# A transformer block on one core: second routing in groups of two tiles, and low weight pieces moved between engines

## The reference

```python
x = x + 0.5 * ffn(layernorm(x), gate, w0, w1, wo)     # first experts
x = x + attention(layernorm(x), ...)                  # 16 heads, latent queries, keys and values, rope
x = x + 0.5 * ffn(layernorm(x), gate, w0, w1, wo)     # second experts, the same weights

logits = x @ gate_kernel                              # 8 experts
w, idx = top_k(logits, 2); w = softmax(w)
inter = silu(x @ w0[e]) * (x @ w1[e])                 # 256 -> 512
out = sum over the two chosen e of w_e * (inter @ wo[e])
```

## Time and profile before

| | us |
|---|---|
| runs | 1121.5, 1124.51, 1124.83 |
| median | 1124.51 |
| profiled execution | 1126.85 |
| its span | 1125.0 |

### The profile page before, as it was taken

One profiled execution on the slowest core, in us unless ns is written; L12 is line 12 of the kernel. 1 busy time (PEld: TensorE's weight loads), 2 busy tenths in 40 slices (PEclk: granted clock), 3 DMA queues, 4 the chain that ended last, 5 costly groups with the idle time before them and its releaser, 6 DMA issues.

```text
span 1125.0 us, 22344 instructions
## 1 busy us (share of the span) xinstructions
PE 1046.2 (93%) x6294; PEld 819.3 (73%) x6295; DVE 714.6 (64%) x1570; ACT 522.0 (46%) x1127; POOL 442.8 (39%) x401
## 2 busy tenths in 40 slices
PE   4669999999889999999999999999989999999994
PEld 4558878887457777777777777777778558788883
DVE  6364665654457788877887887777244645655642
ACT  1243433432156677767677777667201034433321
POOL 2552223333334654645464634443014523223322
PEclk9999999999989999999999999999999899999998
DMA  9843544432100111111101111111644645544230
GB/s 243 269 163 78 134 102 107 103 55 34 57 0 24 44 39 39 38 39 38 34 25 39 38 39 39 38 38 58 216 145 164 205 139 118 146 102 107 45 56 7
DMA packets 71592, 95.82 MB, mean 85 GB/s; under 512 B 9600, under 2 KB 48640, under 8 KB 71296
## 3 DMA queue, kind: packets, MB, share of 16 engines
q1 hardware_dynamic: 57216, 78.04, 22.6%
q0 software_dynamic: 14304, 16.87, 8.7%
HBM read 64.37 MB, written 34.43 MB: 88 GB/s over the span
## 4 chain that ended last, share of the span: by engine, by line
PE 50%; DMA 27%; issue 10%; POOL 3%; DVE 2%; ACT 1%; POOLq 1%; SPq 0%; DVEq 0%; ACTq 0%
DMA out<-shared,small 13%; DMA x_after_moe<-shared,small 13%; PE bank L1632 10%; PE bank L1659 10%; PE bank L1620 5%; PE bank L1621 5%; PE bank L1622 5%; PE bank L1412 2%; PE bank L1607 2%; POOL rows_by_expert L533 2%; PE bank L1608 2%; PE bank L1739 1%; PE bank L1444 1%; PE bank L1446 1%; PE bank L1448 1%
## 5 line engine op out<-in xcount | busy, mean ns | idle before, releaser
L845 ACT ACTIVATE shared<-bank,small 128x512 f32<-128x512 f32 x256 | 176.5, 690 | 92.1 <-DVE small L1266 91.0
L1266 DVE TENSOR_REDUCE small<-bank 128x1 f32<-128x512 f32 x256 | 174.7, 685 | 45.3 <-PE bank L1622 45.0
L777 ACT CAST split_rows_and_inner<-bank 128x512 fp32r<-128x512 f32 x78 | 46.0, 589 | 246.7 <-PE bank L1429 246.7
L1632 PE MATMUL bank<-constants,shared 128*128 128x128 f32 x1024 | 156.1, 275 | 2.2 <-ACT shared L845 0.7
L1632 PEld LDWEIGHTS bank<-constants,shared 128*128 128x128 f32 x1024 | 122.3, 140 | 45.1 <-issue 13.8
L1446 PE MATMUL bank<-expert_weights_low,split_rows_and_inner 128*128 x312 | 143.3, 459 | 0.0
L1448 PE MATMUL bank<-expert_weights_high,split_rows_and_inner 128*128 x312 | 142.3, 456 | 0.0
L1444 PE MATMUL bank<-expert_weights_high,split_rows_and_inner 128*128 x312 | 124.7, 400 | 2.7 <-DVE split_rows_and_inner L1075 2.5
L1080 DVE TENSOR_TENSOR split_rows_and_inner<-bank,split_rows_and_inner 128x512 fp32r<-128x512 f32 x78 | 53.9, 691 | 113.6 <-ACT split_rows_and_inner L777 113.6
L1620 PE MATMUL bank<-expert_weights_high,shared_split 128*128 128x512 f32 x256 | 123.3, 482 | 1.4 <-POOL shared_split L589 1.4
L546 POOL DMA_INDIRECT x_after_moe<-shared,small x39 | 61.6, 1579 | 149.7 <-DMA x_after_moe<-shared,small 114.2
(11 more groups left out here) (189 smaller groups left out, 2165.2 us busy)
## 6 DMA issues: line engine op xcount, KB each, us to landing
expert_weights<-L_ffn_w_kernel SPq DMA_DIRECT2D x32, 512.0 KB, 5.0
shared<-rows_by_expert SPq DMA_DIRECT2D x78, 129.0 KB, 2.1
expert_weights<-L_ffn_wo_kernel SPq DMA_DIRECT2D x16, 512.0 KB, 6.4
shared<-inverse_sums SPq DMA_DIRECT2D x64, 128.0 KB, 2.9
attended_transposed<-shared SPq DMA_DIRECT2D x32, 256.0 KB, 3.1
expert_weights<-x_after_moe SPq DMA_DIRECT2D x8, 512.0 KB, 4.9
expert_weights<-attended_transposed SPq DMA_DIRECT2D x2, 2048.0 KB, 10.1
shared<-attended_transposed SPq DMA_DIRECT2D x2, 2048.0 KB, 11.6
```

The source lines that it names most:

```text
L845: nc.scalar.activation(prob[k % 4], bank[k % 4][:, :], ACT.Exp, bias=negmax[:, k % 8:k % 8 + 1], accum_out=psum[par][:, hh * GT + qt:hh * ...
L1266: V.tensor_reduce(negmax[:, k % 8:k % 8 + 1], bank[k % 4][:, :], AX.X, ALU.max, negate=True).then_inc(max_ready, 1)
L1632: last = tr(bank[4 + k % 2][:, c * P:(c + 1) * P], prob[k % 4][:, c * P:(c + 1) * P], ident)
```

## The change

The second routing goes by groups of two tiles (`GN = (4, 2)`): the transposes of group h and the ranks of the group before stand behind the projection of an even tile, the logits of the group before behind that of an odd one. `x2group` moves from `wraw` into the upper part of `wlo`, so that experts 0 and 1 are loaded as soon as the third group of four tiles is projected. ACT splits expert 0's high pieces around the last group's copies and expert 1's behind its exponential; DVE makes expert 0's low pieces within the last group's steps and expert 1's behind the tables, once the last rows are stored. In both expert stages the low piece of wo of experts 2 to 7 is made by POOL, behind the add before the change of expert. The norm of batch 1 moves behind the first two `ropes`. The counts of `keep_busy` change from 4, 5, 2, 16 to 3, 3, 2, 14. In the diff, slices to the group's size (`[:, 0:n]`) are left out.

```diff
@@ -33,6 +33,7 @@
+GN = (GT, 2)
...
@@ -145,7 +146,9 @@
+        wlo_at = -(-nc.sbuf_base // 32) * 32
+        wlo_plain = nc.alloc_sbuf_tensor_at("expert_weights_low_plain", [P, 2 * WEXP], F32, offset=wlo_at)
...
@@ -285,7 +288,7 @@
-        x2group = [late[:, PAIRS * S + k * GT * D:PAIRS * S + (k + 1) * GT * D].rearrange("p (a n) -> p a n", a=GT)
+        x2group = [wlo_plain[:, 2 * B * S + k * GT * D:2 * B * S + (k + 1) * GT * D].rearrange("p (a n) -> p a n", a=GT)
...
@@ -415,7 +419,7 @@
-                    sp.wait_ge(scattered[f][u], 16 * GT * TOPK * ((NG + 2 - u) // 3))
+                    sp.wait_ge(scattered[f][u], 16 * GN[f] * TOPK * ((NT // GN[f] + 2 - u) // 3))
...
@@ -426,7 +430,8 @@
-                sp.wait_ge(wlo_ready[f], 3)
+                sp.wait_ge(wlo_ready[f], 2)
+                sp.wait_ge(outer_low_ready[f], 1)
...
@@ -438,7 +443,8 @@
-                        sp.wait_ge(wlo_ready[f], e * 3)
+                        sp.wait_ge(wlo_ready[f], e * 2)
+                        sp.wait_ge(outer_low_ready[f], e)
...
@@ -477,7 +483,7 @@
-                    sp.wait_ge(xn_ready[2], g - 1)
+                    sp.wait_ge(xn_ready[2], (g - 1) * GT // GN[1])
...
@@ -505,11 +511,12 @@
                 if g + 2 < NG:
                     load_attended(g + 2)
                     load_x(g + 2)
+                elif g + 2 == NG:
+                    sp.wait_ge(wo_psum, (g + 1) * GT)
+                    load_expert(1, 0)
+                    load_expert(1, 1)
             for u in range(2):
                 sp.wait_ge(out_stored[u], 16 * NG // 2)
-            sp.wait_ge(xn_ready[2], NG)
-            load_expert(1, 0)
-            load_expert(1, 1)
             moe(1)
...
@@ -523,22 +530,33 @@
                 nc.gpsimd.tensor_tensor(rstd[:, bass.ds(at, count)], veps[:, bass.ds(at, count)],
                                         minus_half[:, 0:count], ALU.pow).then_inc(rstd_ready[n], 1)
-            def scatter(f, g):
+            def scatter(f, g, ks=range(TOPK)):
                 u = g % 3
                 pool.wait_ge(slots_ready[f], g + 1)
                 pool.wait_ge(xn_copied[f], g + 1)
-                for k in range(TOPK):
-                    for j in range(GT):
+                for k in ks:
+                    for j in range(GN[f]):
                         nc.gpsimd.indirect_dma_start(
                             out=xs, out_offset=bass.IndirectOffsetOnAxis(ap=slot[u][:, k, j:j + 1], axis=0),
                             in_=rows[u][:, j, k, :], in_offset=None).then_inc(scattered[f][u], 16)
             def add_results(f, dst):
+                def outer_low(e):
+
+                    par = e % 2
+                    pool.wait_ge(whi_ready[f], e * 3 + 3)
+                    nc.gpsimd.tensor_tensor(wlo[:, bass.ds(par * WEXP + 2 * WPIECE, WPIECE)],
+                                            wraw[:, bass.ds(par, 1), 2 * WPIECE:3 * WPIECE].rearrange("p a n -> p (a n)"),
+                                            whi[:, bass.ds(par * WEXP + 2 * WPIECE, WPIECE)].bitcast(F32),
+                                            ALU.subtract).then_inc(outer_low_ready[f], 1)
                 def turn(i):
                     for v in range(3):
+                        last = isinstance(i, int) and i * 3 + v == TILES - 1
+                        if not last:
+                            e = pool.value_load(split_tab[0:1, bass.ds(i * 3 + v + 1, 1)], min_val=0, max_val=E - 1)
                         pool.wait_ge(y_sb[f], i * 3 + v + 1)
                         prev = (v - 1) % 3
                         pool.wait_ge(added[f][prev], (i + (v > 0)) * 16)
...
@@ -548,10 +566,15 @@
                                 ap=tag[v][:, 1:2].bitcast(U32), axis=0),
                             in_=ysb[v], in_offset=None, bounds_check=T - 1, oob_is_err=False,
                             compute_op=ALU.add).then_inc(added[f][v], 16)
-
+                        if not last:
+                            with pool.If(e > 0):
+                                outer_low(e)
+
+                pool.wait_ge(tables_ready[f], 2)
                 turn(0)
-                with pool.Fori(1, TILES // 3) as i:
+                with pool.Fori(1, TILES // 3 - 1) as i:
                     turn(i)
+                turn(TILES // 3 - 1)
             pool.wait_ge(const_in, 48)
             for g in range(NG):
...
@@ -683,13 +706,15 @@
             multiply(NPAIR - 2, 0)
             multiply(NPAIR - 1, 1)
-            pool.wait_ge(veps_ready[2], 1)
-            root(2, 0, GT)
-            for g in range(NG):
-                if g + 1 < NG:
-                    pool.wait_ge(veps_ready[2], g + 2)
-                    root(2, 0, GT)
-                scatter(1, g)
+            for g in range(2):
+                pool.wait_ge(veps_ready[2], g + 1)
+                root(2, 0, GN[1])
+            for g in range(NT // GN[1]):
+                scatter(1, g, (0,))
+                if g + 2 < NT // GN[1]:
+                    pool.wait_ge(veps_ready[2], g + 3)
+                    root(2, 0, GN[1])
+                scatter(1, g, (1,))
             for u in range(2):
                 pool.wait_ge(out_stored[u], 16 * NG // 2)
             add_results(1, out.rearrange("b s d -> (b s) d"))
...
@@ -795,10 +823,6 @@
                             act.wait_ge(y_psum[f], t)
                             split_high(f, e, 2)
-                for e in range(0 if f == 0 else 2):
-                    act.wait_ge(w_in[f], 48 * 2)
-                    for piece in range(3):
-                        split_high(f, e, piece)
                 act.wait_ge(tables_ready[f], 2)
                 expert_steps(act, step)
                 it_high(TILES - 1)
...
@@ -914,10 +938,19 @@
                 pair(p, p % 2)
             take_inverse(NPAIR - 1)
-            for g in range(NG):
+            for g in range(NT // GN[1]):
+                last = g == NT // GN[1] - 1
+                if last:
+                    act.wait_ge(w_in[1], 48 * 2)
+                    split_high(1, 0, 0)
+                    split_high(1, 0, 1)
+                xt_out(2, g, xTr[1], logits_psum[1])
                 copy_rows(1, g)
-                xt_out(2, g, xTr[1], logits_psum[1])
+                if last:
+                    split_high(1, 0, 2)
                 choice_exp(1, g)
+            for piece in range(3):
+                split_high(1, 1, piece)
             moe(1)
...
@@ -944,71 +977,73 @@
-                for j in range(GT):
+                for j in range(GN[n // 2]):
-                dve.wait_ge(scattered[f][g % 3], g // 3 * (16 * GT * TOPK))
+                dve.wait_ge(scattered[f][g % 3], g // 3 * (16 * GN[f] * TOPK))
+                w = GN[n // 2] * P
-                V.tensor_copy(dst[:, 1, :], bank[1][:, :]).then_inc(xn_sb1[n], 1)
+                V.tensor_copy(dst[:, 1, 0:w], bank[1][:, 0:w]).then_inc(xn_sb1[n], 1)
+                u, n = g % 3, GN[f]
-                for j in range(GT):
+                for j in range(n):
-                for j in range(GT):
+                for j in range(n):
+                u, n = g % 3, GN[f]
...
@@ -1067,7 +1102,7 @@
-                                ALU.subtract).then_inc(wlo_ready[f], 1)
+                                ALU.subtract).then_inc((wlo_ready if piece < 2 else outer_low_ready)[f], 1)
...
@@ -1095,6 +1130,13 @@
                     dve.wait_ge(y_psum[f], t + 1)
                     dve.wait_ge(tag_sb[f], t + 1)
                     V.tensor_scalar(ysb[v], bank[7][:, 0:D], tag[v][:, 0:1], None, ALU.mult).then_inc(y_sb[f], 1)
+
+                def second_lows():
+                    if f == 1:
+                        for u in range(2):
+                            dve.wait_ge(out_stored[u], 16 * NG // 2)
+                    for piece in range(3):
+                        split_low(f, 1, piece)
                 def step(i, k):
                     t = i * 3 + k
...
@@ -1113,11 +1155,11 @@
                         scale(t - 1, (k - 1) % 3)
                         with dve.If(e > 0):
                             split_low(f, e, 1)
-                            split_low(f, e, 2)
-
-                for e in range(2):
+
+                if f == 0:
                     for piece in range(3):
-                        split_low(f, e, piece)
+                        split_low(0, 0, piece)
+                second_lows()
                 dve.wait_ge(tables_ready[f], 2)
                 expert_steps(dve, step)
                 it_low(TILES - 1)
...
@@ -1249,7 +1291,6 @@
-            norm_tiles(1, range(GT))
...
@@ -1326,6 +1367,7 @@
             ropes(0, 0)
             ropes(0, 1)
+            norm_tiles(1, range(GT))
             dve.wait_ge(v_kept, 1)
             latent_lower(0, 0, 0)
             latent_lower(0, 0, 1)
...
@@ -1340,30 +1382,36 @@
             own.step(V.memset(carry, 0.0))
             own.settle()
-            def second_route(g, part):
-                if g >= 0:
-                    if part == 0:
```

(101 more changed lines are left out.)

78 lines of the change are left out of this document (42 added, 36 removed).

## The result

The changed kernel took 1109.11 us (median of four runs, 1107.64 to 1109.86), against 1124.26 of the kernel before beside it (four runs): a ratio of 0.9864, 95% interval 0.9844 to 0.9884. The direction was right, and the size was off by 8.7.

The account below looks back on a forecast made before the run. Both expert stages were taken as bound by the chain of DMA adds, the routing between by TensorE, then a serial tail. Terms -9.0 - 0.1 + 2.6 = -6.5 gave 1118.0 us against the median 1124.51; range 1110 to 1125.5.

Parts of the forecast that it names:

- The projection phase: Second routing beside the output projections: groups of two remove TensorE's stalls and the slow tile, -5.8 us.
- The cover of 0.25 us: Each projection period: DVE needs 4.7 us before the norm is ready, TensorE has 4.95 of work, covering the stall.
- rival C: Routing gives less than half: small stalls, late scatter, late zeroes; -4 there, total 1123; chance 0.12.
- The tail: Last projection to second stage's first transposes: slots ready 13.3 us after it; with the projections' gain, transposes come 9.0 earlier.
- The zero rows set the start: Before the second expert stage: SP's zeroing of expert tails, not the scatters, is late, ending 13.0 us after the slots.
- 3.3 + 0.8: Tail, after the zero rows' issue: 3.3 us for the last landing, 0.8 for the register load.
- the three low pieces (3.45): Tail: low weight pieces on DVE's path to the slots, counted as 3.45 us.
- POOL's subtraction: Both expert stages, behind the add at twelve expert changes: POOL's low outer weights delay the next add, +2.6 us.
- The relief of DVE: Both expert stages: DVE loses one of three low pieces, removing 9.5 us of TensorE waits; valued at 0.
- Rival A: Expert stages shorten too: adds follow TensorE, 9.5 us of waits come off; 1106, or 1110 with half; chance 0.1.
- the 35 waits: Second expert stage: 35 of 39 adds waited for the previous landing, 121.3 us; taken as evidence against adds following TensorE.
- The norm: Batch 1's norm moved behind the queries: wins between 0 and 0.2 us, taken as -0.1.

Follow-up runs that it names:

- e8: Changed kernel with ACT issuing four of the eight zero rows and expert 0's low pieces moved behind the tables; 1106.29 us, 0.9833 of the kernel before.
- experiment 7: Changed kernel with 16 instead of 14 filler matmuls before the second expert stage; 1110.28 us, 0.9873 of the kernel before.
- e1: Kernel before with POOL making the low outer weights and nothing else changed; 1120.18 us, 0.9960 of the kernel before.
- e2: Changed kernel with the low outer weights of experts 2 to 7 back on DVE; 1113.48 us, 0.9908 of the kernel before.
- Experiment 1: The pair e1 and e2: POOL's piece alone on the kernel before, 1120.18 us, and the changed kernel with it back on DVE, 1113.48 us.
- experiment 4: Changed kernel without the high-by-low outer product, 4 of TensorE's 36 matmuls per tile, in both expert stages; 1106.30 us, 0.9840 of the kernel before.
- experiment 6: Changed kernel with the norm of batch 1 back ahead of the keys and 4 fillers; 1109.35 us, 0.9868 of the kernel before.
- e3: Changed kernel with nobody making the low outer weights of experts 2 to 7, the semaphore raised without the subtraction; 1106.51 us, 0.9842 of the kernel before.
- e7: Changed kernel with ACT issuing four of the second routing's eight zero rows, leaving SP four; 1107.59 us, 0.9837 of the kernel before.

## Why the prediction was wrong, and where it was right

**The projection phase, right.** -6.7 for -5.8. The stalls of the earlier trace rows and the slow tile are gone. The slow tile was TensorE at a lower granted clock, 0.57, as the kernel before shows:

```profile
844.00:848.00 4.00, 4.00 (x15) 3.32 (x14) 0.69 (x1) 0.93 (x2) 3.09 (x4) 0.57 0.96 333
```

With the stalls in front of it gone the clock stayed at 1.00, as the prediction assumed without naming the clock. The cover of 0.25 us held at every group, and rival C (small stalls, late weights) did not come: ACT's high pieces start at 867.92 without waiting for a load.

**The tail, right, a little better.** The last slots' conversion starts at 877.33 and ends at 877.50, 12.5 behind the last projection (13.3 forecast). The zero rows set the start, as argued, and SP begins them 1.3 later. From the end of their issue to the row loads it is 2.27 where the sum had 3.3 + 0.8, the middle of the earlier trace rows: the lower end was the true one. One term was counted wrongly and did no harm: the three low pieces (3.45) as work on DVE's path, where e8, without them but at a lower granted clock, was no sooner. Not foreseen were the +1.5 behind it: the sum asked whether the fillers lie under the cover, not whether they reach its end, and the gap they left cost TensorE's clock (experiment 7).

**POOL's subtraction, not contradicted.** +2.6 was forecast; 2.6 was measured, not told apart from 0. The duration was 0.5 too short, but the overlap with the add's issue gave 0.56 back. The rule of the Trainium skill (SBUF — State Buffer, on the shared port pair) that spoke against it was not put to the test here: none of the twelve subtractions overlapped one of DVE's low pieces in time.

**The relief of DVE, the step that failed.** The prediction said that "the value of this is 0 while the chain binds". So the relief was put at 0, and the edit at +2.6. Measured, the edit alone made the kernel 4.3 faster (e1), and the changed kernel is 4.4 slower without it (e2): 7.0 of the 8.7 by which the forecast missed. That the adds wait for landings was read as their binding from the fourth tile to the end. What rows 3 and 4 show is a lag of 2.5 in the middle of a stage, and a lag says who is behind there, not who sets the end. Followed to the end, the lag of stage 1 had run down to 1.5 us, with a floor of 0.88: nearly all of a stall of TensorE at a change is paid by the stage. The twelve stalls were 6.5 together, and the stages shortened by about 6. Rows came ready over 189.8 us in stage 1 before and 185.65 after, and the last add with them. Experiment 1 shows it from both sides; experiment 4 shows how small the surplus is, since with TensorE faster the adds bind at the end. Rival A had this mechanism, its place and its price (1106 to 1110, with 1109.1 measured), and was given 0.1, on the strength of the 35 waits. Those are waits in plenty and evidence of nothing but a small surplus: at 4.65 against 4.88 an add chain waits for its landing in nearly every tile and still catches up 0.2 in each. That A's price came out so well is partly luck: the 9.5 counted the two stalls of 1.49 that stayed.

**The norm, right** at nothing.

**The rest of the miss** is smaller and in part the clock: in the profiled pair -2.3 for -0.1 between the stages (experiment 6), -0.9 in the projections, -1.8 and +1.5 in the tail.

**Open** is why stage 2 stays about 1 us longer than stage 1 (means 188.0 and 187.1) and ends with a lag of 2.0 to 2.5, in the kernel before and in the six profiles of the new stages. In the changed kernel's profile one stall of 2.23 explains most of 188.6 against 185.6. e3 reached 186.2 there, and the medians do not tell the two apart.

## What to carry to other kernels

Where two chains of nearly equal pace feed each other, don't count waits: write down the lag between them tile by tile, and look at its value at the end. At its floor, the producer sets the length and every stall of it counts; far above it, the consumer does. Take more than one profile for it: the same code gave stages up to 2 us apart. And when a transfer in front of a stage is made faster, look at what fills the time: fillers that covered it become the bound (e7), or leave a gap that costs clock (the changed kernel).

## What the runs showed of the hardware

POOL's arithmetic started 1.0 us after the start of an indirect DMA that the profile counts as 1.56 us busy, in all twelve places, so the two lie partly over each other. Two of them took 5.33 for 3.00 of one.

The norm at its new place met POOL's arithmetic. DVE's row, then POOL's, of the changed kernel:

```profile
306.57 2.33 DVE L1228 TENSOR_SCALAR expert_weights<-expert_weights,small 128x256 f32<-128x256 f32 x4
```

```profile
306.74 1.37 POOL L603 TENSOR_TENSOR shared<-shared 128x512 f32<-128x512 f32 x1 [3.87 <-DVE shared L1317]
```

The four instructions took 2.33 us where the ones of the earlier trace rows took 1.41. The Trainium skill has a rule for such a pair (SBUF — State Buffer, shared port pair): one of the two is shut out while the other holds the ports. This case's trace agrees, with 0.9 us lost beside 1.37 of POOL: one by one, three of the four took 0.40, and the second, begun 0.15 behind POOL's start, took 1.37 and ended 0.15 behind POOL's end. All eleven profiles with the norm at the new place show the same; the three with it at the old place have 0.40 to 0.41 four times. Nothing waited for it.
